# Work on blocks of 16 steps of all batches beside a recurrence, through output map, attention, shuffle and dense map, in whole-array products

## What is computed

```python
# second layer; x, ctx given by the first one
u = x @ Wi.T + bi;  sp = x @ Ws.T + bs          # L1_attn
state = jnp.tanh(state @ A.T + u_t @ B.T) + sp_t # 256 steps, one after the other
y_t = state @ C.T
x4 = _layernorm(x + ys @ Wo.T + bo)
q = _layernorm(x4 @ wq, ln_gamma, ln_beta)       # L1_xattn, k and v from ctx, 16 heads of 8
q_prime = relu(q) + 1e-6
z = 1 / (q_prime . k_sum + 1e-6)                 # per token and head
att = q_prime @ kv * z                           # (batch, head, token, 8)
att = att.reshape(batch, -1, 128)                # heads are not turned back: a shuffle of rows
x5 = _layernorm(x4 + _layernorm(att @ dense_w + dense_b, ln_gamma, ln_beta))
out = _layernorm(x5 + fp8_product(x5, weight) + bias)  # scale from the largest |x5| of all
```

## Time and profile before

| | us |
|---|---|
| three timed runs | 1171.66, 1177.38, 1177.30 (median 1177.3) |
| the profiled execution, its own time | 1171.73 |
| its span in the profile | 1170.0 |
| recurrence, 895.3 to 1050.8 | 155.5 |
| end of the recurrence to the maximum over x5 | 86.3 |
| maximum to the end | 32.9 |

### The profile page before, as it was taken

The page is one execution under the profiler, slowest core; times in us unless marked ns, Lnnn a source line. Parts: engine busy times, 40 slices in busy tenths (PEclk is TensorE's granted clock), DMA queues, the critical chain, the costliest instruction groups (busy, mean ns, idle before and its releaser), DMA issues.

```text
span 1170.0 us, 19759 instructions
## 1 busy us (share of the span) xinstructions
PE 965.3 (83%) x7491; PEld 646.7 (55%) x7491; DVE 688.5 (59%) x1903; ACT 503.5 (43%) x1398; POOL 464.8 (40%) x532
## 2 busy tenths in 40 slices
PE   3758999999999998999999999998558999996311
PEld 2435656666666666666656666565336655654211
DVE  3346577567758757667675876765562003445598
ACT  3735645654664664555466365433102333331000
POOL 1134466356356546536645644655410001111041
PEclk8789999999999999899999999999858999997655
DMA  6000000000000000000000000000000000010401
GB/s 172 19 1 6 11 1 6 11 1 6 11 1 6 10 1 1 6 10 1 6 10 2 1 1 1 1 19 1 0 1 2 2 1 6 6 8 3 54 0 36
DMA packets 56812, 12.85 MB, mean 11 GB/s; under 512 B 40318, under 2 KB 56462, under 8 KB 56590
## 3 DMA queue, kind: packets, MB, share of 16 engines
q1 hardware_dynamic: 56718, 11.58, 4.7%
HBM read 9.46 MB, written 2.12 MB: 10 GB/s over the span
## 4 chain that ended last, share of the span: by engine, by line
PE 60%; DVE 22%; ACT 6%; POOL 5%; issue 3%; DMA 2%; SPq 1%; POOLq 0%; DVEq 0%
PE score_banks L1611 8%; PE out_bank L1583 7%; PE bank_d L1709 6%; PE bank_a L1371 5%; PE score_banks L1390 5%; DVE o_rec L1082 4%; PE score_banks L1773 4%; DVE prob L1110 3%; PE score_banks L1415 3%; PE bank_d L1466 3%; PE out_bank L1566 3%; PE score_banks L1392 3%; PE score_banks L1391 3%; PE out_bank L1591 2%; DVE stats L919 2%
## 5 line engine op out<-in xcount | busy, mean ns | idle before, releaser
L799 ACT ACTIVATE prob<-score_banks 128x1024 f32<-128x1024 f32 x128 | 131.1, 1024 | 166.0 <-PE score_banks L1611 165.7
L1611 PE MATMUL score_banks<-qh,kr 64*128 64x256 f32 x1024 | 149.2, 411 | 3.0 <-ACT qh L767 2.6
L636 POOL TENSOR_TENSOR psum<-psum,prob 128x512 f32<-128x512 f32 x64 | 81.5, 1274 | 153.7 <-DVE prob L1110 153.6
L546 POOL TENSOR_TENSOR var_eps<-mv,epsilons 128x2 f32<-128x2 f32 (+2 forms) x64 | 12.7, 198 | 314.3 <-DVE mv L922 314.3
L1082 DVE RECIPROCAL o_rec<-out_bank 128x256 f32<-128x256 f32 x64 | 111.9, 1748 | 28.6 <-PE out_bank L1591 28.6
L1583 PE MATMUL out_bank<-prob,v 128*64 128x256 f32 x1024 | 124.6, 385 | 1.3 <-DVE on L1083 1.3
L634 POOL TENSOR_TENSOR psum<-prob 128x512 f32<-128x512 f32 x64 | 83.1, 1298 | 102.6 <-DVE prob L1110 102.6
L1611 PEld LDWEIGHTS score_banks<-qh,kr 64*128 64x128 f32 x1024 | 91.2, 191 | 42.0 <-issue 32.7
L739 ACT ACTIVATE prob<-prob,neg_max 128x128 f32<-128x128 f32 (+1 forms) x256 | 107.0, 425 | 13.0 <-DVE neg_max L982 13.0
L1110 DVE TENSOR_SCALAR prob<-prob 128x1024 f32<-128x1024 f32 x128 | 101.3, 791 | 17.7 <-ACT prob L799 17.7
L1709 PE MATMUL bank_d<-w_qkv_t,ident 128*64 128x192 f32 (+1 forms) x430 | 105.7, 332 | 0.0
(11 more groups left out here) (363 smaller groups left out, 2014.5 us busy)
## 6 DMA issues: line engine op xcount, KB each, us to landing
cb<-in_ctx_dram SPq DMA_DIRECT2D x8, 256.0 KB, 2.9
bias_mask<-bias_scratch SPq DMA_DIRECT2D x1, 1536.0 KB, 7.3
xb<-in_x_dram SPq DMA_DIRECT2D x8, 128.0 KB, 2.1
prob<-in_L_xattn_Wkv_dram SPq DMA_DIRECT2D x1, 1024.0 KB, 6.7
att_scratch<-on SPq DMA_DIRECT2D x16, 64.0 KB, 3.3
prob<-att_scratch SPq DMA_DIRECT2D x2, 512.0 KB, 4.0
out_dram<-v SPq DMA_DIRECT2D x4, 256.0 KB, 2.3
prob<-in_L_xattn_Wq_dram SPq DMA_DIRECT2D x1, 512.0 KB, 7.8
```

The costliest lines, as they stand in the source:

```text
L799: s.activation(prob[:, p % 2, 2 * u:2 * u + 2, :].rearrange("p k (h q) -> p h k q", h=2), sc[:, 0:2, :].rearrange("p h (k q) -> p h k q", ...
L1611: last = mm(sc[:, h, k * T:(k + 1) * T], kr[rows_of, p % 2, kb * P:(kb + 1) * P], qh[rows_of, p % 2, :], start=True, stop=True, skip_group ...
```

## The change

The work behind the recurrence no longer goes by batch in two halves but by window: 16 steps of all 8 batches, 128 tokens that stand side by side in `hid`. There are 16 windows, and each goes the whole way: output map with its bias as a product of one row, norm to x4, query map, norm, scale, shift and ReLU in the turned form, attention, shuffle, dense map, norm, scale and shift. In the diff `window(k, i)` says what PE adds behind step 16 k + i. It works on window k - 1 in slots 0, 1, 7, 9 and 15, on k - 2 in 2 to 5 and 8, on k - 3 in 11 and on k - 4 in 6. `halves` holds one slice over all 128 columns, so every added product uses the whole array. x4 goes to a scratch in HBM and comes back as rows (`x4_rows`), for the residual needs other tokens than the window that was just made. Two more columns are loaded at the start. `ksm` is gone: the sum over a head is a product with `head_mask`. The 16 values of `z` per token are inverted before they are spread over the heads' 8 columns. The bias add and the maximum over x5 go in four parts.

```diff
-            for b in range(B):
-                sp.wait_ge(att_ready, b + 1)
-                store_attended(b, 0)
...
+            for k in range(1, WINDOWS + 2):
+                if k - 1 < WINDOWS:
+                    sp.wait_ge(x4_ready, k)
+                    sp.dma_start(x4_dram[k - 1], x4[:, k - 1, :]).then_inc(x4_out, 16)
+                if k >= 2:
+                    w = k - 2
+                    sp.wait_ge(att_ready, w + 1)
+                    sp.dma_start(att_dram[w], att[:, w, :]).then_inc(att_out, 16)
+                    sp.wait_ge(att_out, 16 * (w + 1))
+                    sp.wait_ge(mixed_in, 16 * w)
+                    sp.dma_start(mixed[:, w, :].rearrange("p (i e) -> p i e", e=HD),
+                                 rows(att_dram, (HD, P), w * P * D, [(B * D, WINDOW_STEPS), (1, HD)]),
+                                 allow_slow_non_contiguous=True).then_inc(mixed_in, 16)
+                if k == WINDOWS - 1:
+                    sp.wait_ge(x4_out, 16 * (WINDOWS - 1))
+                    for b in range(B):
+                        early = slice(H * b, H * b + H - 1)
+                        sp.dma_start(x4_rows[early, :, :], x4_of_batch[b, 0:H - 1]).then_inc(x4_rows_in, 16)
...
+            for k in range(1, WINDOWS + 3):
+                new = k - 1 < WINDOWS
+                if 0 <= k - 2 < WINDOWS:
+                    rectify_queries(k - 2)
+                if new:
+                    dve.wait_ge(pre_full, k)
+                    measure_window(W_X4, bank_d[:, 0:D], x4_var)
+                    dve.wait_ge(x4_rstd, k)
+                    normalize_window(W_X4, x4[:, k - 1, :], bank_d[:, 0:D]).then_inc(x4_ready, 1)
+                if k >= 4:
+                    measure_dense(k - 4)
+                if 0 <= k - 2 < WINDOWS:
+                    divide_attended(k - 2)
...
+            for step, k in ((add_rows, 0), (add_rows, 1), (normalize_x5, 0), (add_rows, 2), (measure_dense, 15),
+                            (normalize_x5, 1), (normalize_dense, 15), (normalize_x5, 2), (add_rows, 3)):
                 step(k)
...
+            def product_of_rows(bank, tokens, weights, **kw):
+                for of in halves:
+                    last = mm(bank[of, 0:D], tokens[:, of], weights, skip_group_check=True, **kw)
+                return last
...
+                q_by_batch = q1_t.rearrange("p (i b) -> p b i", b=B)
+                for b in (2 * part, 2 * part + 1):
+                    for of in halves:
+                        mm(ob[of, 0:P].rearrange("p (i b) -> p b i", b=B)[:, b], kvm[:, b, of], q_by_batch[:, b],
+                           start=True, stop=True, skip_group_check=True)
...
+                if here(k - 1, 0):
+                    inputs_of(k - 1)
+                elif here(k - 1, 1):
+                    states_of(k - 1)
+                elif 2 <= i <= 5 and 0 <= k - 2 < WINDOWS:
+                    attend(k - 2, i - 2)
+                elif here(k - 4, 6):
+                    dense(k - 4)
```

More of the change, by code:

```diff
@@ L669, in _, with rstd_of_window @@
[L669 to L676, removed]
+            def rstd_of_window(at, eps, var, done, count):
+                pool.wait_ge(var, count)
+                link(g.tensor_tensor(var_eps[:, at:at + 1], mv[:, at, 1:2], epsilons[:, EPSILONS.index(eps), 0:1],
+                                     ALU.add))
+                g.tensor_tensor(rstd[:, at:at + 1], var_eps[:, at:at + 1], minus_half[:, 0:1],
+                                ALU.pow).then_inc(done, 1)
@@ new lines, in add_bias @@
+            def add_bias(k):
+                part = slice(4 * k, 4 * k + 4)
+                pool.wait_ge(x5_ready, k + 1)
+                g.tensor_tensor(x2[:, part, :], x5[:, part, :], b_ffn[:, :].unsqueeze(1).broadcast_to([P, 4, D]),
+                                ALU.add).then_inc(x5b_ready, 1)
+            for k in range(3):
+                rstd_of(norms + 8, k, 4, EPS_LN, half=k % 2)
+                if k == 1:
+                    add_bias(0)
+            scale_dense(WINDOWS - 1)
+            finish_dense(WINDOWS - 1)
@@ L1303, in normalize_x5, with measure_window @@
[L1303 to L1311 removed]
+            def measure_window(at, tile, ready):
+                link(w.bn_stats(stats[:, at, :], tile))
+                w.bn_aggr(mv[:, at, :], stats[:, at, :]).then_inc(ready, 1)
@@ L1806, in _, with turn_halves, inputs_of @@
-            for t in range(1, P):
+            halves = [slice(0, P)]
+            def turn_halves(bank, tile):
+                for of in halves:
+                    last = turn(bank[of, 0:P], tile[:, of])
+                return last
+            def product_of_rows(bank, tokens, weights, **kw):
+                for of in halves:
+                    last = mm(bank[of, 0:D], tokens[:, of], weights, skip_group_check=True, **kw)
+                return last
+            def inputs_of(k):
+                if k == 0:
+                    pe.wait_ge(td_free, 9)
+                else:
+                    pe.wait_ge(q_ready, k)
+                product_of_rows(bank_d, x3_t[:, P * k:P * k + P], gws_t, start=True, stop=False)
+                product_of_rows(bank_d, one_row[:, 0:P], bias_row, start=False, stop=False)
@@ L1807, in _ @@
+            for t in range(1, T):
                 step(t)
+                k, i = divmod(t, WINDOW_STEPS)
+                worked = window(k, i)
                 if t <= 3 * Z_PARTS:
                     z_third(*divmod(t - 1, 3))
-                    keep_clock(KEEP_Z)
-                else:
-                    keep_clock()
-            for t in range(P, T):
-                b, i = divmod(t - P, LATE_STEPS)
-                step(t)
-                if i == 0 and b >= 1:
-                    early(b - 1, LATE_STEPS)
-                early(b, i)
-                if i not in PE_EARLY:
-                    keep_clock()
@@ L1821, in _ @@
-            early(B - 1, LATE_STEPS)
-            ja = 9 + B * EARLY_A
-            jd = 9 + B * EARLY_D
-            pe.wait_ge(h_ready, T)
-            groups = [(g, range(g * B // LATE_GROUPS, (g + 1) * B // LATE_GROUPS), (bank_a, ob)[g],
-                       (bank_d, bank_d2)[g], (t4, t4b)[g]) for g in range(LATE_GROUPS)]
-            def turn_four(bank, tiles):
-                for i, tile in enumerate(tiles):
-                    last = turn(bank[:, i * P:(i + 1) * P], tile)
-                return last
@@ L1878, in _ @@
-            ja += 4
-            jd += 4
+                if not worked:
+                    keep_clock(KEEP_Z if t <= 3 * Z_PARTS else KEEP, bank_d2 if t < Z_FIRST // B else sc[:, 0, :])
+            pe.wait_ge(h_ready, T)
+            for t in range(T, T + 4 * WINDOW_STEPS):
+                window(*divmod(t, WINDOW_STEPS))
+            ja = 9
+            jd = 9
             pe.wait_ge(td_free, jd)
```

423 lines of the change are left out of this document (194 added, 229 removed).

## The result

The changed kernel takes 1244.28 us (median of four runs, 1243.22 to 1245.6). The ratio to the kernel before is 1.0574, with a 95% interval of 1.0531 to 1.0617. I had forecast 1141, a range of 1127 to 1160 and "faster", with 0.04 for slower.

What follows compares the result with a forecast made beforehand. Bounds: a PE-ACT round trip in the recurrence, then a chain of engines and DMA. 1171.7 + 16.7 - 51.3 + 0.9 + 0.4 = 1138.4 us, set to 1141 for the spread of earlier runs; range 1127 to 1160.

Steps and rivals of the forecast that it cites:

- the sum for a window: Recurrence: work added to the slots costs 1.78 us per window (1.42 to 2.13), making the recurrence 16.7 us longer, some 172.
- the rival: Recurrence: the clock falls with fewer keep_clock products, 4.5 us more per window, 68 in fifteen, total 1209; chance 0.05.
- Prices of slots at the higher clock: Recurrence: costs beyond a plain step of 0.295 us for two products, 0.075 for one, 0 for turns, 0.215 for attention pairs.
- my middle: Attention slots: pair cost taken as 0.215 us, between 0.135 and 0.295, from rows with passes 0.07 and 0.11 apart.
- the 5.5 that the rule was said to add: Recurrence: by the skill's weight-load rule, attention pairs cost 0.295 and slot 5 0.50, making the sum 5.5 us higher.
- No waits in the windows: Recurrence: no wait counted, tightest slack 0.6 us at slot 2; a rival wait of 15 to 28 us had 0.10.
- The end: From the last Tanh to the maximum over x5: 35 us (31 to 42) instead of 86.3, so 51.3 shorter; DVE's queue decides.
- the end isn't shorter: Stage behind the recurrence: SP issues 16 loads between the last shuffles, DVE waits; 60 us instead of 35, total 1166; chance 0.04.
- The small terms: Start: two more loads, +0.9 us; setup products: one more product and a longer copy, +0.4; last stage: 0.

Runs made afterwards that it cites:

- e7: Changed kernel with a 192-column keep_clock filler in every recurrence slot and a second one in the attention slots: 1221.54 us (one execution).
- e4: Changed kernel without the eight attention products of each window but the first, so the output is not the reference's: 1204.67 us (one execution).
- e8: The kernel before the change, without its keep_clock filler in steps 128 to 255: 1201.6 us (one execution).
- e1: Changed kernel with a keep_clock filler of 192 columns in every slot of the recurrence, those with work too: 1279.3 us (one execution).
- e2: Changed kernel with the 192-column keep_clock filler added in the four attention slots alone: 1275.63 us, ratio 1.0842.
- e10: e6 with the 96-column filler of the worked slots only in slots 1 to 5 and 9: four executions of 1132.05, 1133.87, 1165.56 and 1174.51 us.
- e11: e6 without the filler in slots 0 and 6, where two products stand: 1137.39 us, ratio 0.9655.
- e6: Changed kernel with added products in halves of 64 columns, turns whole, and a 96-column filler in the worked slots: 1138.34 us, ratio 0.9666.
- e3: Changed kernel with every added product cut into two over 64 columns of weights, turns whole, no filler added: 1178.72 us, ratio 1.001.
- e9: e6 with whole-array products instead of halves, the fillers the same: 1293.53 us (one execution).
- e5: e3 with a 192-column filler in every slot: 1162.17 us, ratio 0.9854.

## Why the prediction was wrong

**The step that failed** is the sum for a window. All its prices were taken from rows at the higher clock, and the case in which that clock is lost had 0.05. As a rival it was told with its place and its price: 68 us more in the recurrence, 1209 in all. The runs show that this mechanism happened: the same form with enough filler runs at 1.00 (e7), and the changed kernel ran at 0.50. They also show that it costs more: 263.5 us against the 172 of my sum, 91 more.

About 5 of these 91 are a price that was too low at either clock (next paragraph). The rest is the clock, some 6.3 us per full window (17.51 less the 11.2 estimated below) where the rival had 4.5. The 0.11 per pass that I took for it fits the attention pair, where the passes go from 0.13 to 0.22 apart. What the rival left out is above all the step itself, 0.10 more in each of the 16 slots, 1.6 per window (e4, e8).

Two arguments stood against the rival. That PE is never without work in the windows was worth nothing: PE was busy for 223.6 of 223.6 us at 0.50. That the work slots stood without `keep_clock` before, too, compared 6 slots of 16 with 12 of 16, and e8 shows that the old ones needed the filler of the others.

**Prices of slots at the higher clock.** The attention slot was never seen there without a filler or `z_third`. With one filler it takes 1.08 (e1, window 3), with two 1.41 (e7), so a filler adds 0.33 and about 0.75 remains; I had 0.78. That is an estimate from two kernels. Single products and turns came out as priced, 0.63 (e2) and 0.57 (e10) for 0.64 and 0.57. The slot with two products did not: in the whole-array form it takes 1.05 (e2), where I had 0.86 from the old kernel's products with `kvm` and `ksm`. That is 0.19 in slots 0 and 6 each. In halves it takes 0.85 (e11). With these prices and slot 5 at 0.98 (e1's 1.31 less 0.33) a full window in the whole-array form would take about 11.2 us at 1.00, an estimate, for my 10.8.

The passes of narrow products start further apart than both of my rows had it, 0.07 and 0.11: 0.62 for four passes with records of about 0.23 is 0.13 each. By the Trainium skill's rule of 107 ns for 128 columns (page "TensorE: Matmul & The Clock Gate", section "LDWEIGHTS (loading the stationary operand)"), which I set aside, one gets 0.11; for a pass at the higher clock the trace is nearer to the rule than to my middle of 0.09. At the lower clock a pass takes (1.04 - 0.38) / 3 = 0.22, twice the rule. In the sum, the 5.5 that the rule was said to add is 4.9, 0.35 in each of 14 windows.

**No waits in the windows.** Right. In the changed kernel ACT's Tanh waited for PE alone, 255 times. In e6, at the periods that I had reckoned with, it is the same and a window is 10.29. PE waited for no load of the shuffle in the recurrence of either.

**The end.** Forecast 35 us (31 to 42), measured 43.2 in the changed kernel and 39.2 in e6, against 86.3. The changed kernel lies just outside my bounds. That this stage would shrink by overlap was right; the first row of DVE's queue came late. Chain of the changed kernel:

```profile
1170.84 3.23 PE out_bank L1846 x16
...
1179.82 1.25 issue
1181.06 3.57 PE out_bank L1846 x16
...
1191.73 0.69 DVE bias_mask L1336
...
1197.35 1.44 DVE bias_mask L1336
```

Window 14's attention, which my text named and did not price, lasts 3.7 us at the lower clock (3.23 and 0.43); window 15's lasts 4.0 where I had 3.8. The rows begin 23.1 us behind the last step instead of 17.4. The queue from there to the maximum took 20.1 instead of 17.6. One of its adds takes 1.44 us of the chain where the two before it take 0.69 and 0.59; POOL's bias add of the same size runs beside it, and that this is the cause was not tested. The rival "the end isn't shorter" did not come in its size of 60 us. But its mechanism decides in e6, where PE is done sooner:

```profile
1068.29 7.68 SPq L531 DMA_DIRECT2D bias_mask<-x_scratch  x8
1081.00 6.26 SPq L535 DMA_DIRECT2D bias_mask<-x_scratch  x8
1088.73 0.69 DVE L1336 TENSOR_TENSOR bias_mask<-bias_mask,prob 128x512 f32<-128x512 f32 x1 [0.99 <-DMA bias_mask<-x_scratch]
```

SP issues the 16 loads of x4's rows one after the other, 13.9 us in all, with a store of x4 and window 14's shuffle between the two groups. DVE's first add waits for the last of them, 19.4 us behind the last Tanh. I had let DVE's own queue decide.

**The small terms.** The last stage took 32.1 for 32.9, and the start lies inside the spread of executions. Both are too small to tell.

**What remains without the clock.** e6 takes 1138.3 us, and my sum for the change with the clock kept was 1138.4. That is partly luck: e6 has halves, whose recurrence is 165.1 instead of my 172, and fillers that I had not counted; its end is 4 us longer than my 35. How the changed form would do at 1.00 with no filler at all was not seen; the 11.2 us per window above are an estimate.

**What is settled and what is open.** Between the changed kernel and e6 lie 105.9 us. By way of e3 they divide into 65.6 for the form at the lower clock and 40.4 for the filler that keeps the clock up. By way of e9 the filler alone costs 49.3 and the form then gives 155.2, so neither share is a price of its own. Shown is that a filler holds the clock in halves (e5, e6, e11), that the kernel before loses it without (e8), and that a second filler in the attention slots holds it in the whole form (e7 against e1). The falls of e1 in slots 4 to 6 point to the same slots. e7, e1, e8 and e9 are one execution each, and e10 shows that executions of one kernel can differ by 40 us when the clock falls in some. Open is what in the attention slots brings the clock down, their few moving columns, their shape or the missing filler, and e4 does not settle it. In halves the two falls seen with a filler in the attention slots lie elsewhere, in slot 9 (e11) and slot 11 (e10).

## What to carry to other kernels

Where a small recurrence sets the pace and another kernel's filler products hold TensorE's clock, work that replaces the filler must be priced at the lower clock too, and the first thing to read after such a change is the granted clock by stage. Cut added products into the tile shape that the recurrence itself uses: here a pair of attention products in halves cost nothing beside a step, where the pair on the whole array cost about 0.2 us at the higher clock and 0.6 at the lower. Take no setting that holds the clock only in some executions; e6's filler costs 0.3 us per window more than e11's and the times of both were steady, while e10's were not.

## What the runs showed of the hardware

- In the changed kernel the clock stayed at its lower level for 239 us of recurrence in which PE was busy by the profile all the time. Busy time alone doesn't tell which level will be granted.
- At the lower clock the filler makes things worse: a step takes 0.66 us bare (e4) and 0.85 with 192 columns of filler (free slots of the changed kernel). At the higher clock it takes 0.56 with the filler.
- The clock can return in the middle of such work: in e1 it fell eight times in one recurrence, each time in slots 4 to 6, and rose seven times, in slots 11 to 14.
- Narrow products in two halves of 64 columns: eight passes in 0.59 us against four whole ones in 1.04 at the lower clock, 0.39 against 0.62 at the higher.
- Two products of 128 columns beside a step: the slot takes 1.05 us on the whole array (e2) and 0.85 in halves (e11), both at the higher clock.
- SP needs 7.7 and 6.3 us to issue two groups of eight loads of x4's rows (e6), and in the chain of e6 these issues decide when DVE can begin on the rows.
